# Mamba and LSTM stage: the step size as the larger of two ScalarE paths, and the LSTM cell from sigmoid values

## The reference

```python
dt = jax.nn.softplus(jnp.einsum('blr,cr->blc', dt_in, dw) + db)   # db = -4
A = -jnp.exp(Alog)
def step(h, inp):
    dA = jnp.exp(dt_t[..., None] * A)
    h = dA * h + (dt_t * u_t)[..., None] * B_t[:, None, :]
    y = jnp.einsum('bcn,bn->bc', h, C_t)
...
def step(carry, xt):                                             # LSTM, 33 steps, two directions
    g = xt @ wih.T + h @ whh.T + bih + bhh
    i, f, gg, o = jnp.split(g, 4, axis=-1)
    c = jax.nn.sigmoid(f) * c + jax.nn.sigmoid(i) * jnp.tanh(gg)
    h = jax.nn.sigmoid(o) * jnp.tanh(c)
```

## Time and profile before

| what | value |
|---|---|
| median of 3 runs | 2211.43 us (2204.95 to 2212.78) |
| span of the profiled execution, first to last instruction | 2159.5 us |
| median less span | 51.9 us |
| own time of the profiled execution | not given; the profile shows its span alone |
| stretch of the Mamba and LSTM stage | about 24 to 849 us of the span |

### The profile page before, as it was taken

The page is one execution under the profiler, slowest core; times in us unless marked ns, Lnnn a source line. Parts: engine busy times, 40 slices in busy tenths (PEclk is TensorE's granted clock), DMA queues, the critical chain, the costliest instruction groups (busy, mean ns, idle before and its releaser), DMA issues. The chain is left out here.

```text
span 2159.5 us, 49411 instructions
## 1 busy us (share of the span) xinstructions
PE 1857.5 (86%) x19547; PEld 1357.8 (63%) x19547; DVE 1645.7 (76%) x2609; ACT 1298.3 (60%) x2660; POOL 1011.2 (47%) x775
## 2 busy tenths in 40 slices
PE   7888888889888867897878878889788699999999
PEld 4444444444443323444568877767676599999999
DVE  4999999999999996678465442346554589999897
ACT  5777777777776645114345444252456388888886
POOL 1777777777777773110017777300440033333333
PEclk9999999999999999899679999898899699999999
DMA  3544444444444442520038889501730411112000
GB/s 130 167 132 132 126 137 132 132 132 127 128 139 140 132 137 55 126 45 1 7 100 236 258 257 256 139 1 73 231 114 12 187 64 64 65 65 69 14 7 7
DMA packets 98037, 241.63 MB, mean 112 GB/s; under 512 B 15024, under 2 KB 48320, under 8 KB 95504
## 3 DMA queue, kind: packets, MB, share of 16 engines
q1 hardware_dynamic: 89120, 218.12, 32.7%
q0 software_dynamic: 7680, 15.74, 3.2%
q10 hardware_dynamic: 1008, 4.62, 0.6%
HBM read 226.25 MB, written 12.19 MB: 110 GB/s over the span
## 5 line engine op out<-in xcount | busy, mean ns | idle before, releaser
L1119 POOL TENSOR_TENSOR dBu<-du,Bs 128x858 f32<-128x858 f32 (+1 forms) x240 | 588.2, 2452 | 203.4 <-DVE hst L1046 94.6
L574 PE MATMUL py<-hst,ident 128*128 128x429 f32 (+1 forms) x960 | 416.7, 565 | 95.9 <-DVE hst L1056 95.1
L1046 DVE TENSOR_TENSOR_SCAN hst<-dA,dBu 128x858 f32<-128x858 f32 (+1 forms) x240 | 457.8, 1908 | 17.1 <-ACT dA L889 13.7
L889 ACT ACTIVATE dA<-dt,negA 128x416 f32<-128x416 f32 (+1 forms) x480 | 269.5, 596 | 177.2 <-DVE hst L1046 175.6
L574 PEld LDWEIGHTS py<-hst,ident 128*128 128x128 f32 x960 | 183.6, 202 | 292.3 <-DVE hst L1056 169.0
L3444 POOL TENSOR_TENSOR hm<-h,mw 128x264 f32<-128x264 f32 x128 | 89.7, 701 | 391.0 <-DVE h L3424 391.0
L1056 DVE TENSOR_TENSOR hst<-hst,Cs 128x858 f32<-128x858 f32 (+1 forms) x240 | 246.5, 1027 | 0.0
L3315 PE MATMUL pg<-hs,wh 128*128 128x66 f16 x6144 | 218.8, 194 | 4.8 <-issue 4.7
L3315 PE MATMUL pg<-xm,wi 128*128 128x66 f16 x6144 | 214.6, 195 | 6.8 <-issue 5.4
L3315 PEld LDWEIGHTS pg<-hs,wh 128*128 128x128 f16 x6144 | 204.8, 98 | 8.6 <-issue 5.1
L3315 PEld LDWEIGHTS pg<-xm,wi 128*128 128x128 f16 x6144 | 202.0, 98 | 11.3 <-issue 5.9
(11 more groups left out here) (568 smaller groups left out, 3458.8 us busy)
## 6 DMA issues: line engine op xcount, KB each, us to landing
wb<-sf_w SPq DMA_DIRECT2D x96, 514.0 KB, 4.9
Bs<-bc_rows SPq DMA_DIRECT2D x96, 429.0 KB, 4.6
Cs<-bc_rows SPq DMA_DIRECT2D x96, 429.0 KB, 3.5
mw<-route_weights SPq DMA_DIRECT2D x8, 2112.0 KB, 10.1
wb<-gf_w SPq DMA_DIRECT2D x24, 514.0 KB, 4.9
Bs<-bc_rows SPq DMA_DIRECT2D x24, 396.0 KB, 5.0
Cs<-bc_rows SPq DMA_DIRECT2D x24, 396.0 KB, 4.6
mb<-route_masks SPq DMA_DIRECT2D x8, 1088.0 KB, 5.8
```

What stands on the lines that cost most here:

```text
L574: return nc.tensor.matmul(out, weight, moving, **kw)
L889: last = a(o, by_seq(dt[:, j % 2, h, 0:n])[:, :, 1:S], ACT.Exp, scale=negA[:, l, h * DST + k:h * DST + k + 1])
L1046: v.tensor_tensor_scan(hst[:, g % HR, 0:2 * n], dA[:, g % 2, 0:2 * n], dBu[:, g % 2, 0:2 * n], 0.0, ALU.mult, ALU.add).then_inc(h_ready, 1)
L1119: g_.tensor_tensor(dBu[:, g % 2, 0:2 * n].rearrange("p (a n) -> p a n", a=2), du[:, j % 2, :, 0:n], Bs[:, q % NBS, k % BG, 0:n].unsqueeze( ...
```

## The change

The step size is now `max(pos + ln(e + 1 - 2^-22), low)`. `low` is made on ScalarE alone: the magnitude is cut at 40 by a Relu (`40 - |x|`, not below 0), an Exp of it gives a scaled `exp(-|x|)`, a Square with a bias and a Ln with a bias form a series, and an Exp with scale -0.5 gives the small value back. Abs now goes to a tile of its own, `mag`. VectorE takes the sum and then the larger of the two; the polynomial and the predicated copy are gone. The LSTM's gates get one more ScalarE instruction, `0.5*t + 0.5` over three gates, so that the cell works with sigmoids: one product over two gates, one sum, and a plain product for the output. The halving of `whh` and `fw` is gone. The tables: in items 0 to 10 the one with Exp and Ln is loaded at k = 7 and the one with Exp and Tanh at k = 9; from k = 11 of item 10 on the one with Exp and Ln stays, apart from the Silu of the items 11 and 12.

```diff
-                    a(ser[:, :, 0:n], e[:, :, 0:n], ACT.Square, scale=SER_A, bias=edge[:, 0:1]).then_inc(ser_ready, 1)
-                    a(small[:, :, 0:n], e[:, :, 0:n], ACT.Relu, scale=-4000.0, bias=edge[:, 1:2]).then_inc(marked, 1)
+                    a(low[:, :, 0:n], mag[:, :, 0:n], ACT.Relu, scale=-1.0, bias=edge[:, 4:5]).then_inc(capped, 1)
+                    act.wait_ge(capped, j + 1)
+                    a(low[:, :, 0:n], low[:, :, 0:n], ACT.Exp, scale=-1.0, bias=edge[:, 4:5]).then_inc(w_ready, 1)
+                    act.wait_ge(w_ready, j + 1)
+                    a(low[:, :, 0:n], low[:, :, 0:n], ACT.Square, scale=KAPPA, bias=edge[:, 1:2]).then_inc(sq_w_ready, 1)
...
+            def steps(j, k):
+                if k == 7:
+                    act.wait_ge(sq_w_ready, j + 1)
+                    a(low[:, :, 0:n], low[:, :, 0:n], ACT.Ln, bias=edge[:, 2:3]).then_inc(low_logged, 1)
+                    act.wait_ge(e_ready, j + 1)
+                    a(e[:, :, 0:n], e[:, :, 0:n], ACT.Ln, bias=edge[:, 0:1]).then_inc(ln_ready, 1)
+                if k == 8:
+                    act.wait_ge(low_logged, j + 1)
+                    a(low[:, :, 0:n], low[:, :, 0:n], ACT.Exp, scale=-0.5, bias=edge[:, 3:4]).then_inc(low_ready, 1)
...
                 for g in range(3):
-                    a(act3[:, g, :], pre[:, g, :], ACT.Tanh, scale=0.5, bias=lb[:, 2, g:g + 1])
-                a(cz[:, 0, :], pre[:, 3, :], ACT.Tanh, bias=lb[:, 0, 3:4]).then_inc(gated, 1)
+                    last = a(act3[:, g, :], pre[:, g, :], ACT.Tanh, scale=0.5, bias=lb[:, 2, g:g + 1])
+                last.then_inc(tanhed, 1)
+                a(gc[:, 0, :], pre[:, 3, :], ACT.Tanh, bias=lb[:, 0, 3:4])
+                act.wait_ge(tanhed, t + 1)
+                a(act3, act3, ACT.Identity, scale=0.5, bias=half[:, :]).then_inc(gated, 1)
...
-            a(whh[:, :, :, :], whh[:, :, :, :], ACT.Copy, scale=0.5).then_inc(lw_ready, 1)
-            a(fw[:, 1, :], fw[:, 1, :], ACT.Copy, scale=0.5).then_inc(lw_ready, 1)
...
-                if k == 7 and (j + 1 < NI or j >= 2):
-                    logs(j + 1 if j + 1 < NI else None, j - 2 if j >= 2 else None)
+                if k == 7 and j < LSTM_ITEMS:
+                    nc.scalar.preload_act_table_set("natural_log_exp_and_others")
+                if k in (7, 8) and j + 1 < NI:
+                    steps(j + 1, k)
+                if k == 7 and j >= 2:
+                    logs(j - 2)
+                if k == 9 and j < LSTM_ITEMS:
+                    nc.scalar.preload_act_table_set("exp_and_others")
...
             def soften(j):
                 l, at, n = item(j)
-                dve.wait_ge(ser_ready, j + 1)
-                t = ser[:, :, 0:n]
-                v.scalar_tensor_tensor(out=t, in0=t, scalar=SER_C, in1=e[:, :, 0:n], op0=ALU.add, op1=ALU.mult).then_inc(ser_done, 1)
                 dve.wait_ge(ln_ready, j + 1)
-                dve.wait_ge(marked, j + 1)
-                dve.wait_ge(ser_done, j + 1)
-                v.copy_predicated(ln[:, :, 0:n], small[:, :, 0:n], t).then_inc(patched, 1)
-                dve.wait_ge(patched, j + 1)
                 dve.wait_ge(d_read, 2 * j + 2)
-                v.tensor_tensor(dt[:, j % 2, :, 0:n], pos[:, :, 0:n], ln[:, :, 0:n], ALU.add).then_inc(dt_done, 1)
+                v.tensor_tensor(e[:, :, 0:n], pos[:, :, 0:n], e[:, :, 0:n], ALU.add).then_inc(high_ready, 1)
+                dve.wait_ge(low_ready, j + 1)
+                dve.wait_ge(high_ready, j + 1)
+                v.tensor_tensor(dt[:, j % 2, :, 0:n], e[:, :, 0:n], low[:, :, 0:n], ALU.max).then_inc(dt_done, 1)
...
-                v.scalar_tensor_tensor(out=ig[:, :], in0=act3[:, 0, :], scalar=1.0, in1=cz[:, 0, :],
-                                       op0=ALU.add, op1=ALU.mult).then_inc(prods_ready, 1)
-                v.scalar_tensor_tensor(out=act3[:, 1, :], in0=act3[:, 1, :], scalar=1.0, in1=cz[:, 1, :],
-                                       op0=ALU.add, op1=ALU.mult).then_inc(prods_ready, 1)
-                dve.wait_ge(prods_ready, 2 * t + 2)
-                v.scalar_tensor_tensor(out=cz[:, 1, :], in0=act3[:, 1, :], scalar=0.5, in1=ig[:, :],
-                                       op0=ALU.mult, op1=ALU.add).then_inc(c_ready, 1)
+                v.tensor_tensor(prod[:, :, :], act3[:, 0:2, :], gc[:, :, :], ALU.mult).then_inc(prods_ready, 1)
+                dve.wait_ge(prods_ready, t + 1)
...
+                v.tensor_tensor(gc[:, 1, :], prod[:, 0, :], prod[:, 1, :], ALU.add).then_inc(c_ready, 1)
```

More of the change, by code:

```diff
@@ L421 @@
 HR = 5
-SER_A, SER_B, SER_C = 0.5673937377696069, -0.44049436669574327, 0.8059644831764592
+KAPPA = 2.0 ** -26
+BELOW_ONE = 1.0 - 2.0 ** -22
+CAP = 40.0
+LOG_KAPPA = -26 * 0.6931471805599453
 PER_ITEM = 3
@@ L457, in mamba_lstm @@
         xd = sb("xd", [DTR + 2 * DST + 1, 2, SCW])
+        mag = sb("mag", [128, 2, SCW])
         e = sb("e", [128, 2, SCW])
-        ser = sb("ser", [128, 2, SCW])
-        ln = sb("ln", [128, 2, SCW])
+        low = sb("low", [128, 2, SCW])
         pos = sb("pos", [128, 2, SCW])
-        small = sb("small", [128, 2, SCW], mybir.dt.int8)
         yz = sb("yz", [128, 2, SCW])
@@ L476, in mamba_lstm @@
         fb = sb("fb", [128, 1])
-        cz = sb("cz", [128, 2, NB])
-        ig = sb("ig", [128, NB])
+        half = sb("half", [128, 1])
+        gc = sb("gc", [128, 2, NB])
+        prod = sb("prod", [128, 2, NB])
         tc = sb("tc", [128, NB])
@@ L499, in mamba_lstm @@
             stage(nc, "wop_ready wop_kept cent_ready cent_kept sq_ready var_ready var_kept var_logged rstd_ready m_scaled m_done"))
-        (diag_ready, bias_set, lw_ready, gates_ready, gated, prods_ready, c_ready, tc_ready, r_ready, hs_kept, fused, fused_added) = ctx.enter_context(
-            stage(nc, "diag_ready bias_set lw_ready gates_ready gated prods_ready c_ready tc_ready r_ready hs_kept fused fused_added"))
+        (diag_ready, bias_set, lw_ready, gates_ready, half_set, tanhed, gated, prods_ready, c_ready, tc_ready, r_ready, hs_kept, fused, fused_added) = ctx.enter_context(
+            stage(nc, "diag_ready bias_set lw_ready gates_ready half_set tanhed gated prods_ready c_ready tc_ready r_ready hs_kept fused fused_added"))
         b_loaded = ctx.enter_context(stage(nc, " ".join(f"b_loaded{k}" for k in range(NBS))))
@@ L807, in delta @@
                         act.wait_ge(dt_done, j)
-                    a(e[:, h, 0:n], bank(j, f"d{h}")[:, 0:n], ACT.Abs).then_inc(e_abs, 1)
+                    a(mag[:, h, 0:n], bank(j, f"d{h}")[:, 0:n], ACT.Abs).then_inc(mag_ready, 1)
                     a(pos[:, h, 0:n], bank(j, f"d{h}")[:, 0:n], ACT.Relu).then_inc(d_read, 1)
                 if k == 4:
-                    act.wait_ge(e_abs, 2 * j + 2)
-                    a(e[:, :, 0:n], e[:, :, 0:n], ACT.Exp, scale=-1.0).then_inc(e_ready, 1)
+                    act.wait_ge(mag_ready, 2 * j + 2)
@@ L813, in delta @@
+                    a(e[:, :, 0:n], mag[:, :, 0:n], ACT.Exp, scale=-1.0).then_inc(e_ready, 1)
                 if k == 5:
-                    act.wait_ge(e_ready, j + 1)
-                    a(ser[:, :, 0:n], e[:, :, 0:n], ACT.Square, scale=SER_A, bias=edge[:, 0:1]).then_inc(ser_ready, 1)
-                    a(small[:, :, 0:n], e[:, :, 0:n], ACT.Relu, scale=-4000.0, bias=edge[:, 1:2]).then_inc(marked, 1)
[L818 to L833, removed]
@@ L835, in back, with logs @@
+            def logs(d):
+                l, at, n = item(d)
+                act.wait_ge(var_kept, d + 1)
+                if d >= 1:
+                    act.wait_ge(m_scaled, d)
+                a(rstd[:, 0:n], var[:, 0:n], ACT.Ln, bias=cst["eps"]).then_inc(var_logged, 1)
             def back(j, k):
@@ L905, in _ @@
                 delta(0, k)
-            l, at, n = item(0)
-            a(ln[:, :, 0:n], e[:, :, 0:n], ACT.Ln, bias=1.0).then_inc(ln_ready, 1)
+            for k in (7, 8):
+                steps(0, k)
             act.wait_ge(l_loaded, 112)
-            a(whh[:, :, :, :], whh[:, :, :, :], ACT.Copy, scale=0.5).then_inc(lw_ready, 1)
-            a(fw[:, 1, :], fw[:, 1, :], ACT.Copy, scale=0.5).then_inc(lw_ready, 1)
             act.wait_ge(bias_set, 1)
@@ L920, in _ @@
             decay(2)
-            act.wait_ge(lw_ready, 3)
+            act.wait_ge(lw_ready, 1)
+            act.wait_ge(half_set, 1)
             lstm_gates(0)
@@ L966, in _ @@
                 back(NI - 1, k)
-            logs(None, NI - 1)
+            logs(NI - 1)
             for k in (8, 12):
@@ L1029, in lstm_h @@
                     dve.wait_ge(hs_kept, t - 1)
-                v.scalar_tensor_tensor(out=hr[:, t % 2, :], in0=act3[:, 2, :], scalar=1.0, in1=tc[:, :],
-                                       op0=ALU.add, op1=ALU.mult).then_inc(r_ready, 1)
+                v.tensor_tensor(hr[:, t % 2, :], act3[:, 2, :], tc[:, :], ALU.mult).then_inc(r_ready, 1)
             def fuse(c):
@@ L1096, in build @@
```

(5 more changed lines are left out.)

21 lines of the change are left out of this document (11 added, 10 removed).

## The result

| kernel | median of runs | ratio to the kernel before, 95% interval |
|---|---|---|
| before | 2212.11 us (4 runs, 2204.95 to 2221.88) | |
| changed | 2240.64 us (4 runs, 2231.79 to 2242.12) | 1.0112 (1.0089 to 1.0136) |

The change costs 25 us by the ratio (0.0112 x 2212; the two medians lie 28.5 apart); the forecast was a gain of 8.9 us and the range ended at 2213. It was wrong, and on the other side.

The account below looks back on a forecast made before the run. VectorE was taken to set the pace, with ScalarE's path to `scan(8)` in series. Terms 2.0 - 0.4 - 5.4 - 4.3 - 0.8 = -8.9 us took 2211.4 to 2202.5 us; range 2190 to 2213.

Parts of the forecast that it names:

- The cell: VectorE's LSTM cell: one product and one sum take 0.45 us instead of 0.53, -0.08 each, -0.16 an item.
- soften: VectorE's step size instructions after the scan of k = 8: three plain ones, 3.13 us instead of 4.39, -1.26 us.
- ScalarE at k = 5: Relu, Exp and Square replace Square and mask on ScalarE: 2.97 us instead of 1.80, +1.17 us an item.
- the gates: ScalarE at k = 6: one more Identity over 192 columns, priced at 0.40 us, +0.31 with the overlap.
- k = 7: ScalarE with one table load and three Ln instead of two loads and two Ln: 3.66 us instead of 4.07, -0.41.
- Rival 4: ScalarE's hand-offs cost more than 0.03 us, or a table load comes in at k = 5: 2235 us; chance 0.07.
- rival 2: A table load that leaves k = 7 frees more than its own 1.28 us: 2190 us; chance 0.03.
- The items without LSTM: Items 11 to 13: shorter ScalarE path, soften's 3 x -1.26 and item 12's wait gone, together -4.3 us.
- Item 14: A load of 1.28 us stood before the scan that waited 0.83 us; forecast -0.8 us.
- Ahead of the loop: The step size chain before the first scan runs all in line: +2.1 on ScalarE, -0.1 on VectorE, +2.0 us.
- The two stretches: Each item: `yz` through TensorE and ScalarE to `scan(8)`, lengthened 1.07 us; then VectorE's own to the next `yz`, shortened 1.42.
- rival 3: TensorE's lower clock hits six or more of seven other LSTM items, +9: 2211 us, no change; chance 0.15.

Follow-up runs that it names:

- one product in PSUM: The changed kernel with the forget-gate product written to PSUM, so the cell's sum reads only one operand from SBUF; 0.9962 of the kernel before, 2205.73 us.
- The halves version: Kernel before plus the new step size alone, its ScalarE work done half by half at k = 3 to 5; 0.9912 of the kernel before, 2199.70 us.

## Why the prediction was wrong

**The term that failed is "The cell".** It prices the sum at "0.22 less 0.08 of overlap" by the earlier trace rows. That row's instruction had one operand in PSUM; the new one has both in SBUF, and took 1.136 us in the mean. Instead of -0.08 in each of 33 steps it was +0.83. The place of an operand was not in my accounting at all, none of the rivals held it, and the one rival on the slow side was another mechanism.

With the operand moved the kernel measured 0.9962 against 0.9960 forecast, and that this agrees is partly luck. A second term was put at nothing: the cell at k = 5 "waits some 0.8 us for `gated`; this lies beside ScalarE's path and is not added". In the one profile of that kernel it waited 18.0 us in ten items, 1.8 us each, where the kernel before waited 1.7 us in all:

```profile
DVE ig L1018 <- ACT cz L867: 1.7, 3, 0.7
```

VectorE was busy for 12.9 us less over 800 us (758.76 against 771.62), and the new wait took that back: items 0 to 10 took 590.9 us against 589.9 and 587.1, where the sum had 5.8 us less.

Point by point, for the rest:

- *soften, -1.26 us.* Right: 359.05 to 362.26 is 3.21 us for three instructions, against 4.39; -1.18. The `max` costs 1.053 us. `low` was ready in time: nothing but 0.10 us lies between the sum's end and the `max`.
- *ScalarE at k = 5, the gates, k = 7.* Right to 0.1 us. ScalarE's groups and timeline in the changed kernel:

```profile
L875 ACT ACTIVATE gate_ps<-gate_ps,half 128x192 f32<-128x192 f32 x33 | 13.5, 408 | 0.0
```

```profile
344.34 1.00 ACT L816 ACTIVATE low<-mag,edge 128x858 f32<-128x858 f32 x1
...
345.37 1.01 ACT L818 ACTIVATE low<-low,edge 128x858 f32<-128x858 f32 x1
...
346.41 1.01 ACT L820 ACTIVATE low<-low,edge 128x858 f32<-128x858 f32 x1
347.33 1.12 ACT L897 ACTIVATE dA<-dt,negA 128x416 f32<-128x416 f32 x2
...
351.34 1.28 ACT L955 ACT_TABLE_LOAD   x1
352.63 1.01 ACT L826 ACTIVATE low<-low,edge 128x858 f32<-128x858 f32 x1
353.55 1.00 ACT L828 ACTIVATE e<-e,edge 128x858 f32<-128x858 f32 x1
354.45 0.64 ACT L838 ACTIVATE rstd<-var,eps 128x429 f32<-128x429 f32 x1
355.00 1.12 ACT L897 ACTIVATE dA<-dt,negA 128x416 f32<-128x416 f32 x2
```

  k = 5 is 344.34 to 347.33, 2.99 us (2.97 forecast), with 0.03 us between dependent instructions; the Identity 0.408 (0.40); k = 7 from the load to `decay(8)` 3.66 (3.66). Rival 4 had nothing to stand on.
- *The load.* It frees its 1.28 us and no more; rival 2 fell. The rule beside it, of a drain at every switch of tables (the Trainium skill, "ScalarE: Activation LUTs", "What ACT_TABLE_LOAD costs"), does not agree with the trace here: the load of 351.34 ends at 352.62 and the next activation starts at 352.63.
- *The items without LSTM.* 49.9, 50.4 and 50.1 us against 51.7, 52.2 and 51.2: -4.7 us (-4.3 forecast). Item 14: 42.5 against 43.4, -0.9 (-0.8).
- *Ahead of the loop.* First scan at 48.6 against 46.3 or 46.4: +2.2 (+2.0).
- *The two stretches.* `scan(8)` waits in six of the eleven LSTM items of the changed kernel only, and in eight with one product in PSUM; that the slow sum at k = 1 delays VectorE too and so hides it is likely, not tried; at k = 5 the cell waits for the gates in all eleven, 0.45 to 2.35 us (0.3 to 1.4 forecast). The halves version bears out that ScalarE's path holds VectorE up, but more at the gates than at `scan(8)`, and with a second path to `scan(8)` that I had not seen.
- *TensorE's clock, rival 3.* VectorE's sum at k = 1 stands ahead of `yz`, and TensorE waited for `yz` 27.2 us in the items 1 to 10, against 16.1 before; in item 5 2.16 us where the earlier trace rows has 1.50:

```profile
335.87 2.82 PE L577 MATMUL py<-u,diag 128*128 128x429 f32 x4 [2.16 <-DVE yz L1013]
```

  The diagonal matmuls took 1.9 us or more in seven of the eleven items, against four before, and the granted clock from 335 to 340 us was 0.66, the lower level, 1.2 of 2.4 GHz, in part of it. This cannot be put down to the slow sum: the kernel with one product in PSUM, without a slow sum and with 17 us of waits for `yz`, has seven such items as well, and the kernel before, run again, two. The number of such items changes from one execution of the same kernel to the next, and the clock's part in the loss stays open.

One more thing stays open. The version with one product in PSUM gains 0.38% in 12 runs, 8.4 us, but its one profile shows a loop no shorter than that of before (832.9 against 832.0 and 834.7). The two profiles of before differ by 2.7 us in the loop. In the eleven profiles besides the first the stages behind the loop, which no edit touches, take 1369.8 to 1380.6 us, so single profiles do not resolve 8 us in the whole. Where this kernel's gain arises is not shown.

## What to carry to other kernels

Price an instruction by where its operands lie, not by its shape alone: where GpSimd works most of the time, a VectorE instruction with two operands in SBUF can wait for all that is left of GpSimd's instruction, up to 1.7 us here, and a 64-column one in a serial chain pays that in full. Keep one operand of such small instructions in PSUM, or place them where GpSimd rests. This was seen with float32 `tensor_tensor` and `scalar_tensor_tensor` on VectorE and `tensor_tensor` on GpSimd. Where two paths meet in one wait, shortening one can show nothing until the other is shortened too. And an engine's wait is worth adding up even where it lies beside the path that was looked at.

## What the runs showed that I had not expected

The place of a 128x64 tile, PSUM or SBUF, moves a kernel of 2.2 ms by 1.85%. A 64-column sum took 0.23 us beside an idle GpSimd and up to 1.70 us beside a busy one, and with GpSimd's instruction halved up to 0.97 us; all 24 slow ones ended 0.08 to 0.09 us after an end on GpSimd.
